# A fused attention and expert kernel: the low part of the second w1 moves to GpSimd, that of the first w2 to VectorE, and four row loads go ahead of the next weights

## The chip, the cores and the metric

The kernel runs on one core of a Trainium2 chip. The metric is device time in microseconds (us) of one execution. The kernel before took 206.73 us in the median of three executions (206.60, 206.73 and 295.39). Engines are named as the profile names them: PE is TensorE, with PEld for its weight loads; DVE is VectorE, ACT ScalarE, POOL GpSimd, SP SyncE. SP computes nothing here, it issues transfers.

## What is computed

The reference is one block on x of shape (8, 16, 16, 256): attention along the rows and the columns of each image, then a top-1 mixture of eight experts. The change touches only the second part, which in the reference, cut to its core, is

```
x = x + conv(ln(x), Wq, bq, Wk, bk, Wv, bv, Wo, bo, sigma)    # attention, per image
logits = ln(t) @ wg ; idx = argmax(softmax(logits))           # one expert per token
# each of 8 experts takes its first 256 tokens: di[e] is 256 x 256
h  = relu(einsum('ecm,emh->ech', di, w1))                     # 256 -> 1024
eo = einsum('ech,ehm->ecm', h, w2)                            # 1024 -> 256
out = t + gate * eo, back at the token's place
```

All inputs and outputs are float32. The kernel reaches the accuracy with two numbers of the fp32r type for each operand: a high part, `high = fp32r(w)`, and a low part, `low = w - high`. Each product is then three passes on PE: high by high, high by low, low by high.

## The kernel before

Two stages follow each other.

**Attention.** `sweep` runs over eight images of 256 tokens. At the end of an image POOL scatters its rows (data, gate, token number, scale) with indirect transfers into a table `slots` in device memory, ordered by expert and place (line 426). The last image is written out by hand in the VectorE block (`last_first_tile`, `last_choice`), and its two scatters are the last (`row_last`, `slot_last`).

**Experts.** For expert e the steps are:

- SP loads its 256 rows out of `slots` into `sl` (`load_slots`, line 355; 260 KB). It loads w1 of the expert (1 MB) into the one raw buffer `w1_in_sb`, and w2 (1 MB) into the one raw buffer `w2_in_sb` (lines 360, 362, then 372, 375 in the loop). A load into a raw buffer must wait until both parts of the weights that lie in it are made.
- ACT makes the high parts (`split_w1`, `split_w2`, both line 826), each in two instructions of 128x1024. They wait for the load, `w1_in` or `w2_in`.
- DVE makes the low part of w1 (line 1143) and then counts up `w1_split`; POOL makes the low part of w2 (line 456) and then counts up `w2_split`. Each is two instructions of 128x1024 too.
- DVE normalises the rows (`gathered`, line 1122, tile `xs`), PE transposes them (`gather_T`, line 690), ACT and DVE make high and low parts of the result (lines 863, 1148).
- PE multiplies by w1 (`hidden`): four groups q of two 128-wide columns of h, into four banks of PSUM. ACT makes `h_high` with the relu (line 870) and DVE `h_low` (line 1154), group by group.
- PE multiplies by w2 (`expert_out`), DVE adds the residual (line 1134) and POOL scatters the result rows into `out` (line 478).

High and low buffers are doubled (j is the parity of e); the raw buffers are single. Every engine executes its own stream in the order in which it is written, and semaphores alone tie the engines together. So an instruction that waits holds up all that stands behind it on its engine. The order on PE is: `keep_warm(36)` (line 644, products whose result nobody uses, written between the stages), `gather_T(0)`, `gather_T(1)`, `hidden(0)`, and then for each e: `hidden(e+1)`, `gather_T(e+2)`, `expert_out(e)`. ACT runs for each e the four groups of `hidden(e+1)`, with the high part of w2 of expert e+1 between the second group (q = 1) and the third, and after them the high part of the transposed rows e+2 and of w1 of expert e+2. DVE runs `gathered(e+2)`, the four groups of `hidden_low(e+1)`, `gathered_low(e+2)`, the low part of w1 of expert e+2, `output_rows(e)`.

The raw buffer of w1 is free for its third content (expert 2) when `w1_split` is 2, and that of w2 for its second content (expert 1) when `w2_split` is 1. Experts are counted from 0 in all that follows: the diff's `w2_view[1]` is expert 1.

Of the kernel before, what the change touches and what calls it, by code (L numbers as in the profile page):

```python
# [37 lines left out]
DC = D // P  # L38
NT = N // P
E, F = 8, 1024  # L40
CAP = N // E
FC = F // P
# [42 lines left out]
def wait(eng, sem, value):  # L85

    if isinstance(value, int) and value <= 0:
        return
    eng.wait_ge(sem, value)
# [18 lines left out]
def build(nc, x, Wq, bq, Wk, bk, Wv, bv, Wo, bo, sigma, wg, w1, w2, tables_in, eye, tokens, slots, out):  # L108
    f32, f32r, bf16, i32, u32 = mybir.dt.float32, mybir.dt.float32r, mybir.dt.bfloat16, mybir.dt.int32, mybir.dt.uint32
    ALU, ACT, AX = mybir.AluOpType, mybir.ActivationFunctionType, mybir.AxisListType  # L110

    ctx = ExitStack()
    with ctx:
# [6 lines left out]
        def sem(name):  # L120
            return ctx.enter_context(nc.semaphore(name))
# [12 lines left out]
        w1_in_sb, w2_in_sb = sb("w1_in_sb", [P, DC, F]), sb("w2_in_sb", [P, FC, D])  # L134
# [57 lines left out]
        w1_high, w1_low = ([sb(f"w1_{n}{j}", [P, DC, F], f32r) for j in range(2)] for n in ("high", "low"))  # L192
        w2_high, w2_low = ([sb(f"w2_{n}{j}", [P, FC, D], f32r) for j in range(2)] for n in ("high", "low"))
# [30 lines left out]
        x_in = [sem(f"x_in{j}") for j in range(len(X_GROUPS))]  # L224
        w1_in, w2_in = sem("w1_in"), sem("w2_in")
        w1_high_ready, w1_split, w2_high_ready, w2_split = (sem(n) for n in ("w1_high_ready", "w1_split", "w2_high_ready", "w2_split"))
        row_free, y_free = sem("row_free"), sem("y_free")
        slots_in = [sem(f"slots_in{j}") for j in range(2)]
        x2_stored, x2_stored_last = [sem(f"x2_stored{j}") for j in range(2)], sem("x2_stored_last")
# [45 lines left out]
        def pairs(eng, first, last, body):  # L275

            assert (last - first) % 2 == 1
            with eng.Fori(0, (last - first + 1) // 2) as turn:
                for step in range(2):
                    n = first + step  # L280
                    body(turn + n // 2, n % 2)

        def peeled(n, body, **how):
            body(n // 2, n % 2, **how)
# [20 lines left out]
        @block.sync  # L305
        def _(sp):
            def load_x(g):
                a, b = X_GROUPS[g]
                sp.dma_start(x_sb[:, a:b, :], x_view[:, a:b, :]).then_inc(x_in[g], 16)

            sp.dma_start(wk_sb, matrix(Wk)).then_inc(weights_in, 16)
            load_x(0)
            load_x(1)
            with nc.allow_non_contiguous_dma(reason="bias columns of 128"):
                sp.dma_start(bq_sb[:, :], bq.rearrange("(c p) -> p c", p=P)).then_inc(bq_in, 16)
                sp.dma_start(wg_sb[:, :, :], wg.rearrange("(c p) e -> p c e", p=P)).then_inc(wg_in, 16)
                sp.dma_start(wv_sb, matrix(Wv)).then_inc(wv_in, 16)
                for columns, b in ((bv_sb, bv), (bo_cols, bo)):
                    sp.dma_start(columns[:, :], b.rearrange("(c p) -> p c", p=P)).then_inc(small_in, 16)
            sp.dma_start(table_in[:, :], tables_in).then_inc(const_in, 16)  # L320
            load_x(2)
            sp.dma_start(w1_in_sb[:, :, :], w1_view[0]).then_inc(w1_in, 16)
            for g in range(3, len(X_GROUPS)):
                load_x(g)
            sp.dma_start(token[:, :], tokens).then_inc(token_in, 16)

            sp.sem_inc(row_free, 4)

            sp.wait_ge(xT_made, 1)
            sp.wait_ge(empty_ready, 1)  # L330
            sp.dma_start(slots_view, empty[:, None, :].to_broadcast([P, NT, RW])).then_inc(slots_empty, 16)

            sp.wait_ge(m_ready, 1)
            sp.dma_start(w2_in_sb[:, :, :], w2_view[0]).then_inc(w2_in, 16)

            def store_x2(k, j):
                sp.wait_ge(x2_ready, 2 * k + j + 1)
                sp.dma_start(out_view[:, bass.ds(4 * k + 2 * j, 2), :], row[j][:, :, 0:D]).then_inc(x2_stored[j], 16)
                sp.wait_ge(x2_stored[j], 16 * (k + 1))
                sp.sem_inc(row_free, 1)  # L340
                sp.wait_ge(row_sent[j], 32 * (k + 1))
                sp.sem_inc(row_free, 1)

            peeled(0, store_x2)

            sp.wait_ge(w1_split, 1)
            sp.dma_start(w1_in_sb[:, :, :], w1_view[1]).then_inc(w1_in, 16)
            pairs(sp, 1, B - 2, store_x2)

            sp.wait_ge(row_sent_last, 32)  # L350

            def load_slots(k, j):

                wait(sp, slots_in[j], 16 * k)
                sp.dma_start(sl[:, bass.ds(4 * k + 2 * j, 2), :], slots_view[:, bass.ds(4 * k + 2 * j, 2), :]).then_inc(slots_in[j], 16)

            peeled(0, load_slots)
            peeled(1, load_slots)
            sp.wait_ge(w1_split, 2)
            sp.dma_start(w1_in_sb[:, :, :], w1_view[2]).then_inc(w1_in, 16)  # L360
            sp.wait_ge(w2_split, 1)
            sp.dma_start(w2_in_sb[:, :, :], w2_view[1]).then_inc(w2_in, 16)
            pairs(sp, 2, E - 1, load_slots)

            sp.sem_inc(y_free, 2)

            def load_weights(k, j, w1_too=True):


                e = 2 * k + j  # L370
                sp.wait_ge(w2_split, e)
                sp.dma_start(w2_in_sb[:, :, :], w2_view[e]).then_inc(w2_in, 16)
                if w1_too:
                    sp.wait_ge(w1_split, e + 1)
                    sp.dma_start(w1_in_sb[:, :, :], w1_view[e + 1]).then_inc(w1_in, 16)
                sp.wait_ge(y_sent[j], 32 * k)
                sp.sem_inc(y_free, 1)

            pairs(sp, 2, E - 3, load_weights)
            peeled(E - 2, load_weights)  # L380
            peeled(E - 1, load_weights, w1_too=False)
            for j in range(2):
                sp.wait_ge(y_sent[j], 32 * (E // 2))
# [3 lines left out]
        def _(pool):  # L387
# [63 lines left out]
            def split_w2(n, j):  # L451

                for part in range(2):
                    pool.wait_ge(w2_high_ready, 2 * n + part + 1)
                    half = slice(part * FC // 2, (part + 1) * FC // 2)
                    step = nc.gpsimd.tensor_tensor(w2_low[j][:, half, :], w2_in_sb[:, half, :], w2_high[j][:, half, :].bitcast(f32), ALU.subtract)  # L456
                step.then_inc(w2_split, 1)
# [4 lines left out]
            peeled(B - 1, rstd2)  # L462
            peeled(B - 2, scatter_rows, tiles=[1])
            peeled(B - 1, scatter_rows)
            split_w2(0, 0)

            for j in range(2):
                pool.wait_ge(x2_stored[j], 16 * (B // 2 - j))  # L470
            pool.wait_ge(x2_stored_last, 16)
# [20 lines left out]
        def _(pe):  # L492
# [213 lines left out]
            def expert_out(k, j, last=False):  # L706

                e = 2 * k + j
                pe.wait_ge(w2_split, e + 1)
                pe.wait_ge(h_split, (FC // 2) * (e + 1))  # L710
                for t in range(2):
                    own = slice(t * P, (t + 1) * P)
                    step = three_passes(ps_y_last[t] if last else ps_y[j][:, t, :],
                                        [(h_high[j][:, f, own], h_low[j][:, f, own]) for f in range(FC)],
                                        [(w2_high[j][:, f, :], w2_low[j][:, f, :]) for f in range(FC)])
                    if last or t == 1:
                        step.then_inc(y_made, 1)
# [8 lines left out]
            peeled(0, gather_T)  # L726
            peeled(1, gather_T)
            peeled(0, hidden)
            pairs(pe, 0, E - 3, expert)
            peeled(E - 2, expert, two_on=False)  # L730
            pe.wait_ge(y_ready[1], E // 2 - 1)
            peeled(E - 1, expert_out, last=True)
# [3 lines left out]
        def _(act):  # L736
# [91 lines left out]
            def split_w1(n, j):  # L828
                split_w(w1_high, w1_in, w1_in_sb, w1_high_ready, n, j)

            def split_w2(n, j):
                split_w(w2_high, w2_in, w2_in_sb, w2_high_ready, n, j)
# [23 lines left out]
            act.wait_ge(x2_ready, B)  # L856
            act.dma_start(out_view[:, NT - 2:NT, :], row_last[:, :, 0:D]).then_inc(x2_stored_last, 16)
            peeled(B - 1, gate_exp)
            split_w2(0, 0)

            def gathered_T(k, j):
# [17 lines left out]
                    gathered_T(k + 1, j)  # L879
                    split_w1(e + 2, j)  # L880

            split_w1(1, 1)
            peeled(0, gathered_T)
            peeled(1, gathered_T)
            peeled(0, hidden)
# [5 lines left out]
        def _(dve):  # L891
# [247 lines left out]
            def split_w1(n, j):  # L1139

                for c in range(DC):
                    dve.wait_ge(w1_high_ready, DC * n + c + 1)
                    step = nc.vector.tensor_tensor(w1_low[j][:, c, :], w1_in_sb[:, c, :], w1_high[j][:, c, :].bitcast(f32), ALU.subtract)  # L1143
                step.then_inc(w1_split, 1)
# [72 lines left out]
            peeled(B - 1, place)  # L1217
            peeled(B - 1, finish_rows)

            split_w1(1, 1)  # L1220
            for n in range(2):
                peeled(n, gathered)
            for n in range(2):
                peeled(n, gathered_low)
            peeled(0, hidden_low)
            pairs(dve, 0, E - 3, expert)
            peeled(E - 2, expert, two_on=False)
            peeled(E - 1, output_rows, last=True)
# [23 lines left out]
```

## Time and profile before

| What | us |
|---|---|
| median of three executions, and the other low one | 206.73, 206.60 |
| span of the profiled execution, first to last instruction | 204.0 |
| PE busy, share of the span | 185.1 (91%) |
| VectorE busy | 146.6 (72%) |
| ScalarE busy | 105.4 (52%) |
| GpSimd busy | 102.8 (50%) |
| mean granted clock of TensorE, share of full speed | 0.961 |
| attention stage, to the last products of the last image | 0 to 89.6 |
| products of `keep_warm` between the stages | 89.6 to 100.8 |
| expert stage on PE | 102.0 to 198.6 |

The profile covers one execution. Its own device time is not listed apart from the three times; the two low ones stand 2.6 and 2.7 us over the span, and this remainder (launch and end) is taken as the same for both kernels. Of the span the profile gives the busy time of each engine, the instructions in order of time, what each idle stretch of an engine waited for, and the clock that was granted to TensorE. A row of the timeline reads: start, duration, engine, line, operation, tile written and tiles read, number of instructions merged, and in brackets the idle time ahead of it and who ended it. Two matmul instructions are issued for one float32 product, so counts of `keep_warm` are 72 for 36 products.

### The profile page before, as it was taken

Reading aid. Unit: us, or ns where it says so; the run is one execution under the profiler, and the core shown is the slowest. Engines: PE = TensorE matmul, PEld = TensorE weight load, DVE = VectorE, ACT = ScalarE, POOL = GpSimd, SP = SyncE. Lnnn points to the kernel's source line nnn. Section 1 sums busy time; section 2 is a strip of 40 time slices with the busy share of each in tenths; the row PEclk is TensorE's granted clock in tenths of the full one; section 3 lists DMA queues with packets and bytes.
Section 4 is the critical chain, followed back from the end, with each engine's and each line's share of the span. In section 5 each row is a group of like instructions: output and inputs, shape, how many; then the busy total and the mean of one; then the engine's idle time right before and its main releaser. Section 6 shows DMA issues by size and latency. Waiting matters only on the chain.

```text
span 204.0 us, 4341 instructions
## 1 busy us (share of the span) xinstructions
PE 185.1 (91%) x1404; PEld 176.7 (87%) x1404; DVE 146.6 (72%) x460; ACT 105.4 (52%) x246; POOL 102.8 (50%) x101
## 2 busy tenths in 40 slices
PE   7799399999999985959799999999999999999990
PEld 7699399998798883849789999999999999999980
DVE  0579998898999999776956584866858496465510
ACT  2368367888678644235043927538192653826000
POOL 3327574246456357558400636639183663918351
PEclk9999889999999999676999999999999999999997
DMA  5799750103712211331387639192753909271010
GB/s 186 210 394 346 223 193 0 56 0 72 292 51 83 69 60 53 105 127 51 104 310 240 178 105 345 32 367 79 235 228 113 348 16 345 96 205 42 3 55 33
DMA packets 23294, 30.86 MB, mean 151 GB/s; under 512 B 2559, under 2 KB 20113, under 8 KB 23280
## 3 DMA queue, kind: packets, MB, share of 16 engines
q1 hardware_dynamic: 20704, 25.81, 38.5%
q0 software_dynamic: 1616, 4.02, 5.5%
q10 hardware_dynamic: 960, 0.85, 1.2%
q8 instruction: 7, 0.11, 0.2%
q14 instruction: 7, 0.06, 0.1%
HBM read 22.57 MB, written 8.45 MB: 152 GB/s over the span
## 4 chain that ended last, share of the span: by engine, by line
PE 64%; DVE 22%; issue 5%; DMA 3%; ACT 2%; SPq 1%; POOLq 1%; POOL 1%; DVEq 0%; ACTq 0%
PE banks_v L506 7%; PE banks_v L513 7%; PE banks_v L507 7%; DVE w_low L1143 4%; PE bank_q L513 3%; PE bank_pT L513 3%; PE bank_pT L506 3%; PE bank_pT L507 3%; DMA wg_sb<-in_L_ffn_wg 3%; PE bank_q L506 3%; PE bank_s L513 3%; PE bank_s L506 3%; PE bank_s L507 3%; PE bank_q L507 3%; PE banks_o L580 2%
## 5 line engine op out<-in xcount | busy, mean ns | idle before, releaser
L456 POOL TENSOR_TENSOR w_low<-w_in_sb,w_high 128x1024 fp32r<-128x1024 f32 x16 | 38.4, 2421 | 17.1 <-ACT w_high L826 16.8
L478 POOL DMA_INDIRECT out<-y,goal x16 | 15.7, 979 | 35.5 <-DVE y L1134 29.1
L826 ACT ACTIVATE w_high<-w_in_sb 128x1024 fp32r<-128x1024 f32 x32 | 31.9, 1052 | 1.4 <-DMA w_in_sb<-in_L_ffn_w 1.4
L1143 DVE TENSOR_TENSOR w_low<-w_in_sb,w_high 128x1024 fp32r<-128x1024 f32 x14 | 28.1, 2044 | 4.5 <-ACT w_high L826 4.3
L426 POOL DMA_INDIRECT slots<-row,slot x14 | 14.2, 1016 | 18.1 <-DVE slot L1086 16.1
L870 ACT ACTIVATE h_high<-bank_xT 128x512 fp32r<-128x512 f32 x8 | 4.8, 597 | 28.5 <-PE bank_xT L513 28.5
L644 PE MATMUL bank_xT<-ones_wide 128*128 128x128 f32 x100 | 17.8, 360 | 1.1 <-DVE ones_wide L893 1.1
L580 PE MATMUL banks_o<-v_sb,pT 128*128 128x264 f32 x64 | 18.1, 411 | 0.6 <-DVE logit L1021 0.5
L644 PEld LDWEIGHTS bank_xT<-ones_wide 128*128 128x128 f32 x100 | 17.2, 272 | 1.1 <-DVE ones_wide L893 1.1
L506 PE MATMUL banks_v<-w_high,h_high 128*128 128x256 f32 x64 | 15.9, 287 | 0.0
L507 PE MATMUL banks_v<-w_high,h_low 128*128 128x256 f32 x64 | 15.7, 283 | 0.0
L1154 DVE SCALAR_TENSOR_TENSOR h_low<-bank_s,h_high 128x512 fp32r<-128x512 f32 x8 | 5.5, 691 | 12.6 <-ACT h_high L870 12.6
L506 PE MATMUL bank_pT<-w_high,h_high 128*128 128x256 f32 x56 | 13.9, 287 | 0.0
L507 PE MATMUL bank_pT<-w_high,h_low 128*128 128x256 f32 x56 | 13.7, 283 | 0.0
L580 PEld LDWEIGHTS banks_o<-v_sb,pT 128*128 128x128 f32 x64 | 11.5, 198 | 2.2 <-issue 0.7
L506 PE MATMUL banks_v<-m_high,xT_high 128*128 128x272 f32 x32 | 9.9, 324 | 3.4 <-DVE m_low L914 3.4
L507 PEld LDWEIGHTS banks_v<-w_high,h_low 128*128 128x128 f32 x64 | 12.3, 192 | 0.0
L506 PEld LDWEIGHTS banks_v<-w_high,h_high 128*128 128x128 f32 x64 | 12.3, 192 | 0.0
L396 POOL TENSOR_TENSOR rstd<-var_eps,minus_half 128x2 f32<-128x2 f32 (+1 forms) x6 | 4.8, 808 | 14.4 <-DVE var_eps L911 14.4
L747 ACT ACTIVATE xn<-sl,nmr,rstd 128x256 f32<-128x256 f32 (+1 forms) x16 | 8.7, 593 | 4.5 <-POOL nmr L398 4.4
L507 PEld LDWEIGHTS bank_pT<-w_high,h_low 128*128 128x128 f32 x56 | 10.7, 191 | 0.0
L506 PEld LDWEIGHTS bank_pT<-w_high,h_high 128*128 128x128 f32 x56 | 10.7, 191 | 0.0
(200 smaller groups left out, 614.5 us busy)
## 6 DMA issues: line engine op xcount, KB each, us to landing
w_in_sb<-in_L_ffn_w SPq DMA_DIRECT2D x16, 1024.0 KB
slots<-empty SPq DMA_DIRECT2D x1, 2080.0 KB, 13.7
sl<-slots SPq DMA_DIRECT2D x8, 260.0 KB, 3.2
out<-row SPq DMA_DIRECT2D x7, 256.0 KB
sl<-in_x SPq DMA_DIRECT2D x4, 256.0 KB, 6.0
sl<-in_x SPq DMA_DIRECT2D x2, 512.0 KB, 8.8
table_in<-in_tables SPq DMA_DIRECT2D x1, 292.0 KB, 6.3
w_in_sb<-in_L_conv_Wq ACTq DMA_DIRECT2D x1, 256.0 KB, 3.5
```

What stands on the lines that cost most here:

```text
L426: nc.gpsimd.indirect_dma_start(slots, bass.IndirectOffsetOnAxis(ap=slot_of(k, j)[:, t:t + 1].bitcast(u32), axis=0), row_of(k, j)[:, t, :], ...
L456: step = nc.gpsimd.tensor_tensor(w2_low[j][:, half, :], w2_in_sb[:, half, :], w2_high[j][:, half, :].bitcast(f32), ALU.subtract)
L478: nc.gpsimd.indirect_dma_start(out_rows, bass.IndirectOffsetOnAxis(ap=goal[j][:, c:c + 1].bitcast(u32), axis=0), y[j][:, c, :], None, boun ...
L506: nc.tensor.matmul(out_ap, a_h, b_h, start=c == 0, stop=False)
L507: nc.tensor.matmul(out_ap, *second, start=False, stop=False)
L513: step = nc.tensor.matmul(out_ap, *third, start=False, stop=c == n - 1)
L580: step = nc.tensor.matmul(ps_o[:, t, 0:VW], pT[:, c, t * P:(t + 1) * P], v_sb[j][:, c, :], start=c == 0, stop=c == 1)
L644: nc.tensor.matmul(ps_xT[:, 0, 0:P], ones_wide[:, :], ones_wide[:, :], start=True, stop=True)
L747: step = nc.scalar.activation(xn[:, t, :], x_sb[:, bass.ds(r, 1), :], ACT.Identity, scale=rstd[:, bass.ds(r, 1)], bias=nmr[:, bass.ds(r, 1)])
L826: nc.scalar.activation(high[j][:, half, :], raw[:, half, :], ACT.Copy).then_inc(ready, 1)
L1143: step = nc.vector.tensor_tensor(w1_low[j][:, c, :], w1_in_sb[:, c, :], w1_high[j][:, c, :].bitcast(f32), ALU.subtract)
L1154: nc.vector.scalar_tensor_tensor(h_low[j][:, 2 * q:2 * q + 2, :], ps_h[q], 0.0, h_high[j][:, 2 * q:2 * q + 2, :].bitcast(f32), ALU.max, AL ...
```

## The change

Five things change; nothing that is computed does, and no buffer is added.

1. ACT makes the high part of w1 of expert 1 ahead of the high part of w2 of expert 0 (it was the other way round).
2. POOL makes the low part of w1 of expert 1 (`second_w1_low`) in the place where it made the low part of w2 of expert 0.
3. DVE no longer makes the low part of w1 of expert 1. It makes the low part of w2 of expert 0 (`first_w2`), behind `hidden_low(0)` and ahead of its loop over the experts. A semaphore of its own, `first_w2_low`, tells of it, and `w2_split` counts from expert 1 on.
4. SP issues four loads of rows, not two, ahead of the weights of the next experts, and waits for `first_w2_low` before it loads w2 of expert 1.
5. PE has the first two turns of its expert loop written out, since expert 0 waits for another semaphore; the loop has two turns of two experts left.

```diff
-            peeled(0, load_slots)
-            peeled(1, load_slots)
+            for n in range(4):
+                peeled(n, load_slots)
             sp.wait_ge(w1_split, 2)
             sp.dma_start(w1_in_sb[:, :, :], w1_view[2]).then_inc(w1_in, 16)
-            sp.wait_ge(w2_split, 1)
+            sp.wait_ge(first_w2_low, 1)
             sp.dma_start(w2_in_sb[:, :, :], w2_view[1]).then_inc(w2_in, 16)
-            pairs(sp, 2, E - 1, load_slots)
+            pairs(sp, 4, E - 1, load_slots)
...
-                sp.wait_ge(w2_split, e)
+                sp.wait_ge(w2_split, e - 1)
...
-            split_w2(0, 0)
+            def second_w1_low():
+                for c in range(DC):
+                    pool.wait_ge(w1_high_ready, DC + c + 1)
+                    step = nc.gpsimd.tensor_tensor(w1_low[1][:, c, :], w1_in_sb[:, c, :], w1_high[1][:, c, :].bitcast(f32), ALU.subtract)
+                step.then_inc(w1_split, 1)
+            second_w1_low()
...
-                pe.wait_ge(w2_split, e + 1)
+                if isinstance(e, int) and e == 0:
+                    pe.wait_ge(first_w2_low, 1)
+                else:
+                    wait(pe, w2_split, e)
...
-            pairs(pe, 0, E - 3, expert)
+            peeled(0, expert)
+            peeled(1, expert)
+            pairs(pe, 2, E - 3, expert)
...
+            split_w1(1, 1)
             split_w2(0, 0)
...
-            split_w1(1, 1)
             peeled(0, gathered_T)
...
-            split_w1(1, 1)
+            def first_w2():
+                for part in range(2):
+                    dve.wait_ge(w2_high_ready, part + 1)
+                    half = slice(part * FC // 2, (part + 1) * FC // 2)
+                    step = nc.vector.tensor_tensor(w2_low[0][:, half, :], w2_in_sb[:, half, :], w2_high[0][:, half, :].bitcast(f32), ALU.subtract)
+                step.then_inc(first_w2_low, 1)
...
             peeled(0, hidden_low)
+            first_w2()
             pairs(dve, 0, E - 3, expert)
```

The streams at the places that matter are these. First SP, from the end of the attention stage on, before the change (`sl<-slots` are the loads of rows; of the weights 128x2x1024 is a w1 and 128x8x256 a w2):

```order
L355 DMA sl<-slots 128x2x260 [waits row_sent_last]
L355 DMA sl<-slots 128x2x260
L360 DMA w_in_sb<-in_L_ffn_w 128x2x1024 [waits w1_split]
L362 DMA w_in_sb<-in_L_ffn_w 128x8x256 [waits w2_split]
L278 UNCONDITIONAL_BRANCH
L278 ISA
L355 ISA [waits slots_in0]
L355 DMA sl<-slots 128x2x260
```

And the same place with the change:

```order
L356 DMA sl<-slots 128x2x260 [waits row_sent_last]
L356 DMA sl<-slots 128x2x260
L356 DMA sl<-slots 128x2x260 [waits slots_in0]
L356 DMA sl<-slots 128x2x260 [waits slots_in1]
L361 DMA w_in_sb<-in_L_ffn_w 128x2x1024 [waits w1_split]
L363 DMA w_in_sb<-in_L_ffn_w 128x8x256 [waits first_w2_low]
L279 UNCONDITIONAL_BRANCH
L279 ISA
L356 ISA [waits slots_in0]
L356 DMA sl<-slots 128x2x260
```

The rows of experts 2 and 3 have moved ahead of both weight loads, and the load of w2 waits for another semaphore than before.

Second DVE, behind the last slot numbers of the attention stage, before the change:

```order
L1086 SCALAR_TENSOR_TENSOR slot_last<-place_of,over 128x2 [waits place_step]
L1143 TENSOR_TENSOR w_low<-w_in_sb,w_high 128x1024 [waits w1_high_ready] x2
L1122 TENSOR_SCALAR xs<-sl 128x256 [waits slots_in0]
L1122 TENSOR_SCALAR xs<-sl 128x256
L1122 TENSOR_SCALAR xs<-sl 128x256 [waits slots_in1]
L1122 TENSOR_SCALAR xs<-sl 128x256
L1148 TENSOR_TENSOR xg_low<-banks_o,xg_high 128x512 [waits gT_ready] x2
```

With the change, the same place and on to the loop (which begins with the branch of line 279):

```order
L1096 SCALAR_TENSOR_TENSOR slot_last<-place_of,over 128x2 [waits place_step]
L1132 TENSOR_SCALAR xs<-sl 128x256 [waits slots_in0]
L1132 TENSOR_SCALAR xs<-sl 128x256
L1132 TENSOR_SCALAR xs<-sl 128x256 [waits slots_in1]
L1132 TENSOR_SCALAR xs<-sl 128x256
L1158 TENSOR_TENSOR xg_low<-banks_o,xg_high 128x512 [waits gT_ready] x2
L1164 SCALAR_TENSOR_TENSOR h_low<-bank_xT,h_high 128x512 [waits h_high_ready]
L1164 SCALAR_TENSOR_TENSOR h_low<-bank_q,h_high 128x512 [waits h_high_ready]
L1164 SCALAR_TENSOR_TENSOR h_low<-bank_s,h_high 128x512 [waits h_high_ready]
L1164 SCALAR_TENSOR_TENSOR h_low<-banks_v,h_high 128x512 [waits h_high_ready]
L1235 TENSOR_TENSOR w_low<-w_in_sb,w_high 128x1024 [waits w2_high_ready] x2
L279 UNCONDITIONAL_BRANCH
```

The pair of w_low instructions has gone from ahead of `xs`; another pair stands behind the four groups of `h_low` of expert 0.

Third ACT, in its expert loop. This place does not change, but the second row here waits for the load that SP now issues elsewhere:

```order
L881 ACTIVATE h_high<-bank_q 128x512 [waits h_made]
L832 ISA
L836 ACTIVATE w_high<-w_in_sb 128x1024 [waits w2_in]
L836 ACTIVATE w_high<-w_in_sb 128x1024
L880 REGISTER_ALU
L881 ACTIVATE h_high<-bank_s 128x512 [waits h_made]
L880 REGISTER_ALU
L881 ACTIVATE h_high<-banks_v 128x512 [waits h_made]
L873 ISA
L874 ACTIVATE xg_high<-banks_o 128x512 [waits gT_made]
L832 ISA
L836 ACTIVATE w_high<-w_in_sb 128x1024 [waits w1_in]
```

It reads: the high part of w2 of the next expert, then the third and fourth group of h, the transposed rows, and the high part of w1. The order is as before.

## Rows read from the trace of the kernel before

**Rows 1.** The chain of waits between the stages: start, duration, what.
```profile
90.87 2.85 ACT w_high L826 x3
...
93.75 7.50 DVE w_low L1143 x2
101.25 0.66 DVE xs L1122 x2
```

**Rows 2.** Timeline of PE from `keep_warm` to `hidden` of expert 2.
```profile
89.62 11.21 PE L644 MATMUL bank_xT<-ones_wide 128*128 128x128 f32 x72
101.95 1.30 PE L690 MATMUL banks_o<-ident,xs 128*128 128x128 f32 x8 [1.12 <-DVE xs L1122]
...
109.39 0.28 PE L506 MATMUL bank_xT<-xg_high,w_high 128*128 128x256 f32 x1
...
115.50 0.36 PE L506 MATMUL banks_v<-w_high,h_high 128*128 128x256 f32 x1
...
121.34 0.30 PE L506 MATMUL bank_xT<-xg_high,w_high 128*128 128x256 f32 x1
```

**Rows 3.** The tile w_low, 88 to 150 us: duration in ns, min/median/max.
```profile
L456 POOL TENSOR_TENSOR w_low<-w_in_sb,w_high x9: 2384/2421/2435, 94.3 to 150.0; 128x1024 fp32r<-128x1024 f32 x9
L1143 DVE TENSOR_TENSOR w_low<-w_in_sb,w_high x8: 1210/1524/6367, 93.7 to 143.8; 128x1024 fp32r<-128x1024 f32 x8
```

**Rows 4.** Timeline of POOL: low parts of w2, experts 0 and 1.
```profile
94.28 4.75 POOL L456 TENSOR_TENSOR w_low<-w_in_sb,w_high 128x1024 fp32r<-128x1024 f32 x2
114.09 4.81 POOL L456 TENSOR_TENSOR w_low<-w_in_sb,w_high 128x1024 fp32r<-128x1024 f32 x2 [15.06 <-ACT w_high L826]
```

**Rows 5.** Timeline of SP, the issues; then from issue to landing of the row loads.
```profile
96.17 0.91 SPq L355 DMA_DIRECT2D sl<-slots  x2
...
101.69 0.47 SPq L362 DMA_DIRECT2D w_in_sb<-in_L_ffn_w  x1
...
119.08 0.38 SPq L372 DMA_DIRECT2D w_in_sb<-in_L_ffn_w  x1
121.29 0.38 SPq L375 DMA_DIRECT2D w_in_sb<-in_L_ffn_w  x1
...
178.68 0.37 SPq L372 DMA_DIRECT2D w_in_sb<-in_L_ffn_w  x1
...
DMA to landing us min/median/max: 2.7/3.2/7.6
```

**Rows 6.** Timeline of DVE: last h_low of expert 0, then low part of w1, expert 2.
```profile
110.22 0.69 DVE L1154 SCALAR_TENSOR_TENSOR h_low<-banks_v,h_high 128x512 fp32r<-128x512 f32 x1 [0.75 <-ACT h_high L870]
...
117.41 3.71 DVE L1143 TENSOR_TENSOR w_low<-w_in_sb,w_high 128x1024 fp32r<-128x1024 f32 x2
```

**Rows 7.** Timeline of ACT: w2 of expert 1, then w2 and w1, one expert later.
```profile
112.96 2.00 ACT L826 ACTIVATE w_high<-w_in_sb 128x1024 fp32r<-128x1024 f32 x2
...
124.92 2.00 ACT L826 ACTIVATE w_high<-w_in_sb 128x1024 fp32r<-128x1024 f32 x2
...
129.00 2.01 ACT L826 ACTIVATE w_high<-w_in_sb 128x1024 fp32r<-128x1024 f32 x2 [0.61 <-DMA w_in_sb<-in_L_ffn_w]
```

**Rows 8.** Busy time by stretch, the last w2 load: stretch, engines, PEclk, DMA share, GB/s.
```profile
179.50:181.00 1.50, 1.50 (x15) 1.50 (x14) 1.45 (x3) 0.00 (x0) 0.00 (x0) 1.00 0.85 136
181.00:182.50 1.50, 1.50 (x15) 1.50 (x14) 0.88 (x2) 0.00 (x0) 0.00 (x0) 1.00 1.01 354
...
183.00:183.50 0.50, 0.50 (x7) 0.50 (x6) 0.14 (x1) 0.33 (x1) 0.31 (x1) 1.00 0.74 240
```

**Rows 9.** The same view around two idle stretches of PE (first engine column).
```profile
20.40:23.86 3.46, 0.03 (x2) 0.00 (x1) 3.46 (x3) 1.88 (x6) 2.75 (x1) 1.00 0.99 300
23.86:27.50 3.64, 3.64 (x17) 3.64 (x18) 3.54 (x17) 0.68 (x3) 1.41 (x3) 0.53 0.64 202
...
86.90:89.40 2.50, 0.07 (x1) 0.00 (x0) 2.40 (x16) 0.23 (x2) 1.07 (x2) 0.91 0.32 111
...
89.40:95.70 6.30, 6.24 (x33) 6.25 (x34) 2.94 (x10) 4.46 (x8) 5.10 (x5) 0.50 0.29 100
```

More of the change, by code:

```diff
@@ L226, in build @@
         w1_high_ready, w1_split, w2_high_ready, w2_split = (sem(n) for n in ("w1_high_ready", "w1_split", "w2_high_ready", "w2_split"))
+        first_w2_low = sem("first_w2_low")
         row_free, y_free = sem("row_free"), sem("y_free")
```

## The prediction, as written before the result

> **What bounds the kernel now.** I read the chain of waits first. Through the experts it is PE, one matmul behind the other. Between the stages it leaves PE: four small ACT instructions, ACT's high parts of both weights, 7.50 us of DVE on two low parts, then `xs`, then the transposes [rows 1]. So the change works on a stretch of the chain. The timeline of PE tells how much lies there: the products of `keep_warm` run from 89.62 to 100.83, and only the 1.12 us behind them are idle [rows 2]. The reader should see that the chain names DVE for 7.50 us, while PE has other work in its stream for all but 1.12 of them.
>
> Why DVE takes 7.50 us is in the tile's view: one of its low parts takes 1.21 us at best and 6.37 at most [rows 3]. The long one began at 93.75 and POOL's two instructions ran from 94.28 to 99.03 [rows 4]: DVE got on only when POOL was through. Later it is alike: the pair that began at 117.41 ended at 121.12, 2.22 us after POOL's pair ended at 118.90 [rows 6, 4]. I reckon 2.4 us for a pair of DVE that is alone, and 2.2 us past the end of POOL's pair for one that meets it.
>
> **The head of the expert stage.** Without the pair on DVE, `xs` waits only for the rows. Their loads are issued at 96.17 and land 2.7 to 3.2 us later at the usual, so at 98.9 to 99.4 [rows 5]. Two `xs` take 0.66 us on the chain, so they are ready by 100.1. PE is free at 100.83 and no sooner, since `keep_warm` stays. Gain: 101.95 - 100.83 = **1.1 us**. It would be 0 if the rows landed at 101.2 or later (the longest landing shown, 7.6 us, is of a load that ran beside two weight loads), and it can't exceed 1.12.
>
> POOL's pair costs as much on w1 as on w2, the same shape, 4.75 us: `w1_split` is 2 at 99.0, not 101.25, and PE needs it for `hidden(1)`, which began at 109.39 [rows 2] and would now at 108.3. Free. The swap of ACT's high parts costs nothing: three of the four are done by 93.72 [rows 1], the fourth about 1 us later, and nothing but POOL's pair waits there. The row loads of experts 2 and 3 ahead of w1 of expert 2 put that load at about 100; before, it went out just ahead of the w2 at 101.69 [rows 5], so it is not late. PE's two written-out turns add rows to its stream and no matmul; no row prices them, and I take 0, since the loop's turns already join without a gap in the same timeline.
>
> **The load of w2 of expert 1: the term that decides.** Before, it was issued at 101.69 [rows 5] and ACT read it at 112.96 [rows 7], 11.3 us later. Now the raw buffer is free only when `first_w2` is done, and that stands behind `hidden_low(0)`. Its last group ran from 110.22 to 110.9 [rows 6]; with the 1.1 us of the head, to 109.8. Add a DVE pair alone, 2.4 us: SP issues the load at **112.2**. ACT comes to its wait after q = 1, at 112.96 - 1.1 = 111.9. The load cannot be there: it isn't even issued.
>
> How long does 1 MB take from issue to landing? Below: the last w2 was issued at 178.68 [rows 5], and its data flow until close to 183.5, first at 136 GB/s, then at 354, and still at 240 in the half microsecond from 183.0 [rows 8]; so not under 4.7 us. Above: w1 of expert 3, issued at 121.29 behind a w2, ended ACT's wait at 129.00 [rows 5, 7], 7.7 us. Between: w2 of expert 2, issued at 119.08, was there when ACT read it at 124.92 without a wait, so in 5.84 us at most. I take 5.8, since that is the same kind of load, and now 0.5 MB of rows for experts 4 and 5 are issued right behind. Landing at **118.0**.
>
> The Trainium skill (DMA: Bandwidth & Descriptors, Anatomy of one DMA) gives about 2.0 us fixed and the bytes by 436 GB/s; for 1 MB that makes 4.4 us as an estimate, and the result would be 1.4 us lower than mine. Rows 8 speak against it, with data still moving 4.3 to 4.8 us after the issue, and the measurement decides.
>
> **What is queued behind the wait.** On ACT, behind the high part of w2, stand the third and fourth group of `h_high`, the transposed rows, and the high part of w1 of expert 2. DVE's low part of that w1 needs it, and `hidden(2)` on PE needs that. POOL's low part of w2 of expert 1 starts as soon as ACT has its first half, so it collides with DVE's pair, as before. All this is one pattern, and its length is in the trace: ACT began w2 at 112.96 and DVE ended the low part of w1 at 121.12 [rows 7, 6], 8.2 us. PE started `hidden(2)` at 121.34, at once behind `expert_out(0)` [rows 2], so 0.2 us was all the slack there was. Now: 118.0 + 8.2 = **126.2**. PE has `hidden(1)`, `gather_T(2)` and `expert_out(0)` until 121.34 - 1.1 = 120.2 (`expert_out(0)` began at 115.50 [rows 2], now at 114.4, and `first_w2` is done at 112.2: free). PE then stands idle for **6.0 us**. Net against before: 126.2 - 121.34 = **+4.9 us**. With the load's bounds, +3.8 to +6.8.
>
> Behind that the old rhythm returns, late by this sum: the w2 load of expert 2 is issued when POOL is done, 2.3 us before `hidden(2)` starts, as before, and DVE's `y_free` has been given by then.
>
> **The clock.** After PE idled for 3.4 us (20.4 to 23.86) the next 3.6 us ran at a mean of 0.53, after 2.5 us (86.9 to 89.4) the next 6.3 us at 0.50 [rows 9]: the lower of its two levels, 1.2 GHz instead of 2.4. So I expect the same behind 6.0 us of idle. What it costs is half of the slow stretch: 3.4/2 = 1.7 us or 6.3/2 = 3.15 us. Neither row is nearer, I take the middle, **2.4 us**. PE is the bound there, so nothing hides it.
>
> **Sum.** The profiled execution has 204.0 us of span; 204.0 + 4.9 + 2.4 = 211.3, and with the 2.7 us around the span **214.0 us**, 3.5% slower. 204.0 + 2.7 is 206.7, the median of the three runs, so one sum serves for both. The bounds of the two unknown costs together give 206.7 + 3.8 + 1.7 = 212.2 to 206.7 + 6.8 + 3.15 = 216.7.
>
> **Rivals.**
> - *The wait comes, the clock stays.* PE loses only the 6.0 us of idle: 211.6 us, at the load's bounds 210.5 to 213.5. For it: nothing in the rows; against it: both idle stretches ahead of slow ones, and shorter ones at that [rows 9]. 0.07.
> - *Not slower: the load is hidden.* The head's 1.1 us is all that is left, 205.6 us. The place is ACT's wait at q = 1. With the price of the clock at 1.7 us, the kernel would be within 2% (4.1 us) of before only if the load landed within 3.4 us of its issue, and it would gain only if ACT's wait were over by 113.0, 0.8 us after the issue. Against it stand the 4.7 us of rows 8, and DVE's order, which puts `first_w2` behind h_low. 0.05.
> - *The transfers pile up.* The row loads of experts 4 and 5 run beside w2 of expert 1, and the later weight loads, issued in the same spacing, lose their small slack (ACT waited 0.61 us for one already [rows 7]). Then the landing takes 7.7 us or more and a wait or two of 0.5 to 1 us follow: 216 to 218 us. 0.12. The Trainium skill (DMA: Bandwidth & Descriptors, Queues, rings and completion order) says that each DMA engine consumes the descriptors of a ring in order, so rows issued behind w2 should not delay it; by that this rival would not come, and no row here shows a load that was issued alone ahead of rows.
> - *The change does not do what it says at the head.* The rows land late or `xs` meets POOL's pair, and PE starts no sooner: 214.0 + 1.1 = 215.1 us. POOL's pair ends at 99.0, before the rows are there, which speaks against it. 0.08.
>
> My forecast has 0.68. The range should leave out 2 in 10: it runs from the lower case with the clock up, 210.6, to the piled-up transfers, 216.9. A measurement of this kernel can tell about 2% from no change, that is 202.6 and 210.9. Slower than that: the forecast, the head and the pile-up in full, and most of the case with the clock up: 0.92. Within 2%: the hidden load and the rest, 0.07. Faster by over 2% would need 4.1 us, and only 1.1 us of idle is there to remove: 0.01.
>
> **What would show it.** (1) PE's transposes of expert 0 start at about 100.8, directly behind `keep_warm`. (2) DVE's pair of w_low between 109.8 and 112.2, with 1.2 us for each. (3) SP issues w2 of expert 1 at about 112.2; ACT has a wait of about 6 us for it between the second and third group of expert 1, ended by the transfer. (4) PE is idle for about 6 us before `hidden(2)`, ended by DVE's w_low, and the granted clock is 0.5 for 3 to 6 us behind it. (5) From there on every expert takes the 11.96 us of before (112.96 to 124.92 on ACT [rows 7]). The forecast falls if the load lands in under 4 us, or if POOL's pair and DVE's don't meet (then `hidden(2)` comes up to 1.5 us sooner).

## The result

The changed kernel is slower: 213.18 us in the median (212.91 to 215.20), the kernel before 206.71 on the same chip, a ratio of 1.0295 with an interval of 1.0224 to 1.0366. I had forecast 214.0 us and a ratio of 1.035. Each ratio in this document is estimated from those executions of both kernels that lie near their fastest, so it need not be the quotient of the medians. Executions of one kernel spread by 1 to 2%: the changed kernel from 212.91 to 215.20, the kernel before, on another chip, from 205.78 to 210.13. In the one kernel that was profiled twice, most of the difference lies in the attention stage, where TensorE's granted clock was low for longer in one of the two (see the first experiment). So the argument below goes by stretches of one profiled execution, and the times are given beside them.

Three numbers of each profile carry it. The first product of `keep_warm` between the stages marks the end of attention on PE. From there to the first transpose of the expert stage is the *head*. From that transpose to the end of the span is the *expert stretch*.

| Kernel | keep_warm starts | head | expert stretch | span |
|---|---|---|---|---|
| before | 89.62 | 12.33 | 102.05 | 204.0 |
| changed | 90.54 | 9.99 | 110.47 | 211.0 |
| difference | +0.92 | -2.34 | +8.42 | +7.0 |

The expert stretch lost 8.4 us and the head gave 2.3 back. The 0.9 us ahead of both is attention, where nothing was changed. The spans differ by 7.0 us and the medians by 6.5, most likely because the span of 204.0 does not belong to an execution of 206.7 us: in all 33 executions of the kernel before for which the record has both numbers, on other chips, the time is 1.74 to 1.88 us over the span, not 2.7.

**PE.** This is the timeline of PE in the changed kernel; the lines of the second stage are shifted, line 690 of before is 695. It answers to [rows 2].

```profile
90.54 9.90 PE L649 MATMUL bank_xT<-ones_wide 128*128 128x128 f32 x72
100.53 1.42 PE L695 MATMUL banks_o<-ident,xs 128*128 128x128 f32 x8
...
118.97 1.12 PE L518 MATMUL banks_v<-w_low,h_high 128*128 128x256 f32 x8
125.69 0.58 PE L511 MATMUL bank_xT<-xg_high,w_high 128*128 128x256 f32 x1 [5.60 <-DVE w_low L1153]
```

The transposes now stand right behind `keep_warm`, 0.09 us later. Between `expert_out` of expert 0 and `hidden` of expert 2, where 121.34 had followed without a gap, PE is idle for 5.60 us and DVE's w_low ends it.

**The chain.** The chain of waits (start, duration, what) says what DVE waited for in its turn. It answers to [rows 1].

```profile
96.96 2.75 DMA sl<-slots
99.73 0.73 DVE xs L1132 x2
...
110.55 1.23 DVE w_low L1235
111.80 5.71 DMA w_in_sb<-in_L_ffn_w
...
118.50 1.04 ACT w_high L836
...
124.42 1.22 DVE w_low L1153
125.69 0.58 PE bank_xT L511
```

Read it from the bottom: PE waits for DVE's low part of w1, that for ACT, ACT for the transfer, the transfer for VectorE's `first_w2` (line 1235). In the kernel before no transfer stood in this part. ACT's and POOL's timelines show the same wait from their side:

```profile
111.06 0.60 ACT L881 ACTIVATE h_high<-bank_q 128x512 fp32r<-128x512 f32 x1 [0.84 <-PE bank_q L518]
117.53 2.01 ACT L836 ACTIVATE w_high<-w_in_sb 128x1024 fp32r<-128x1024 f32 x2 [5.88 <-DMA w_in_sb<-in_L_ffn_w]
...
120.88 2.01 ACT L836 ACTIVATE w_high<-w_in_sb 128x1024 fp32r<-128x1024 f32 x2
```

```profile
95.21 4.74 POOL L470 TENSOR_TENSOR w_low<-w_in_sb,w_high 128x1024 fp32r<-128x1024 f32 x2
118.67 4.75 POOL L457 TENSOR_TENSOR w_low<-w_in_sb,w_high 128x1024 fp32r<-128x1024 f32 x2 [18.72 <-ACT w_high L836]
```

Compare the pair of ACT at 117.53 with [rows 7]: w2 of expert 1 began at 112.96 without a wait on a transfer, now at 117.53 after 5.88 us. The rest of the pattern is a copy: POOL's pair starts 1.14 us behind it, as it did before, 114.09 against 112.96 [rows 4, 7].

**The clock.** Busy time by stretch: the columns are those of [rows 8], the first number behind the stretch's length is PE.

```profile
120.10:125.70 5.60, 0.01 (x1) 0.01 (x1) 5.57 (x7) 2.79 (x4) 3.32 (x2) 0.91 0.35 105
125.70:131.30 5.60, 5.60 (x26) 5.60 (x27) 2.13 (x6) 0.68 (x2) 1.97 (x2) 0.50 1.03 356
131.30:132.30 1.00, 1.00 (x10) 1.00 (x10) 0.45 (x1) 1.00 (x2) 0.00 (x0) 0.91 0.33 132
```

After 5.6 us of idle PE works for 5.6 us at 0.50, the level of 1.2 GHz: 26 matmuls in 5.6 us, where the next microsecond alone has 10. That costs 5.6/2 = 2.8 us. With the idle time it is 8.4 us, which is all that the expert stretch lost.

### The profile page after: what moved, and what is told of

It is laid out like the page before. It is cut to its first block, busy times and chain, and to the rows that moved or that the text cites. A ratio compares the mean times of both kernels' runs of the same rounds, so it can differ in the third digit from the quotient of the medians.

```text
span 211.0 us, 4318 instructions
## 1 busy us (share of the span) xinstructions
PE 186.5 (88%) x1404; PEld 177.1 (84%) x1404; DVE 139.9 (66%) x460; ACT 106.5 (50%) x246; POOL 102.8 (49%) x101
## 4 chain that ended last, share of the span: by engine, by line
PE 52%; DVE 22%; DMA 9%; issue 8%; POOL 3%; ACT 3%; DVEq 1%; SPq 1%; POOLq 1%; ACTq 0%
PE banks_v L518 5%; PE banks_v L511 5%; PE banks_v L512 5%; DVE prob L1012 4%; DMA wg_sb<-in_L_ffn_wg 3%; PE bank_pT L518 3%; PE bank_pT L511 3%; PE bank_pT L512 3%; PE bank_q L511 3%; DMA w_in_sb<-in_L_ffn_w 3%; PE bank_q L518 3%; PE bank_q L512 3%; PE bank_s L511 2%; PE bank_s L512 2%; PE bank_xT L511 2%
## 5 line engine op out<-in xcount | busy, mean ns | idle before, releaser
L457 POOL TENSOR_TENSOR w_low<-w_in_sb,w_high 128x1024 fp32r<-128x1024 f32 x14 | 33.6, 2420 | 23.6 <-ACT w_high L836 23.6
L1153 DVE TENSOR_TENSOR w_low<-w_in_sb,w_high 128x1024 fp32r<-128x1024 f32 x12 | 19.5, 1659 | 2.9 <-ACT w_high L836 2.7
L585 PE MATMUL banks_o<-v_sb,pT 128*128 128x264 f32 x64 | 17.5, 399 | 0.6 <-DVE logit L1031 0.5
L649 PE MATMUL bank_xT<-ones_wide 128*128 128x128 f32 x100 | 15.4, 327 | 1.1 <-DVE ones_wide L903 1.1
L649 PEld LDWEIGHTS bank_xT<-ones_wide 128*128 128x128 f32 x100 | 15.0, 242 | 1.1 <-DVE ones_wide L903 1.1
L511 PE MATMUL bank_xT<-xg_high,w_high 128*128 128x256 f32 x32 | 9.2, 308 | 5.6 <-DVE w_low L1153 5.6
L585 PEld LDWEIGHTS banks_o<-v_sb,pT 128*128 128x128 f32 x64 | 11.0, 189 | 2.2 <-issue 0.7
L512 PEld LDWEIGHTS banks_v<-w_high,h_low 128*128 128x128 f32 x64 | 12.3, 192 | 0.0
L511 PEld LDWEIGHTS banks_v<-w_high,h_high 128*128 128x128 f32 x64 | 12.3, 192 | 0.0
L511 PEld LDWEIGHTS bank_xT<-xg_high,w_high 128*128 128x128 f32 x32 | 6.6, 206 | 6.0 <-DVE w_low L1153 5.8
L1132 DVE TENSOR_SCALAR xs<-sl 128x256 f32 (+1 forms) x16 | 5.9, 408 | 7.8 <-DMA sl<-slots 7.7
```

The lines of the kernel that those rows point to most:

```text
L511: nc.tensor.matmul(out_ap, a_h, b_h, start=c == 0, stop=False)
L512: nc.tensor.matmul(out_ap, *second, start=False, stop=False)
L585: step = nc.tensor.matmul(ps_o[:, t, 0:VW], pT[:, c, t * P:(t + 1) * P], v_sb[j][:, c, :], start=c == 0, stop=c == 1)
L649: nc.tensor.matmul(ps_xT[:, 0, 0:P], ones_wide[:, :], ones_wide[:, :], start=True, stop=True)
```

## The experiments

All start from the changed kernel. "Before" is always the kernel before on the same chip, 207.7 to 208.1 us in the median. The changed kernel itself was not run on those chips, so the experiments are compared with it by the ratio and by the expert stretch.

### The first w2's low part earlier

```diff
-            peeled(0, hidden_low)
             first_w2()
+            peeled(0, hidden_low)
```

> The changed kernel, with one move: VectorE makes the first w2's low part ahead of the four groups of h_low of expert 0, not behind them. My theory (the loss is ScalarE's wait for the load of w2 of expert 1, plus the slow clock behind TensorE's idle time): the pair now ends near 105.6, the load is issued there, lands 5.7 us later at 111.3, ScalarE asks at 111.6, so nobody waits and TensorE never idles; the time is 205.6 to 206.5 us, at or just under the kernel before. Rival A (the loss is VectorE's extra pair as such, or TensorE's two written-out turns): both are still there, so most of the 6.5 us stays, 211 to 213 us.

It took 206.91 us in the median, before 207.96. One execution took 203.38 us and three 206.62 to 207.35, too few to tell more, so I repeated it.

> The run with the first w2's low part ahead of h_low, repeated, since it had but one undisturbed time (203.38 us). My theory: the whole loss is the late issue, so this is 205 to 206.5 us, 0.5 to 2.5 us under the kernel before on the same chip. Rival A (VectorE's extra pair or TensorE's written-out turns cost by themselves): 208 us or more.

Measured: 203.54 us (202.95 to 207.37), before 207.74, ratio 0.9804 with an interval of 0.9745 to 0.9863. The ten executions of this kernel fall into two groups, five from 202.95 to 203.80 us and five from 206.62 to 207.37, and the ratio speaks of the lower group. The first profile is of the upper group (207.35 us) and the second of the lower (203.15). Their spans differ by 4.3 us, and 3.5 of them are attention, which ends at 92.70 and at 89.18: in the first the granted clock was 0.51 from 11 to 21 us, in the second 1.00. Where it matters the two agree: the expert stretch is 102.13 and 102.03 us, that of before is 102.05. This is the timeline of SP and then of ACT in the second one:

```profile
104.12 0.38 SPq L363 DMA_DIRECT2D w_in_sb<-in_L_ffn_w  x1
```

```profile
110.18 2.00 ACT L836 ACTIVATE w_high<-w_in_sb 128x1024 fp32r<-128x1024 f32 x2
```

The load has 6.06 us and ACT does not wait. All 8.4 us are gone while VectorE's extra pair and TensorE's two written-out turns are still there: neither costs anything here, and rival A falls. From the start of `keep_warm` to the end this version takes 112.0 and 112.8 us in its two profiles, the kernel before 114.4 and the changed kernel 120.5. So it is about 8 us shorter there than the changed kernel and 1.6 to 2.4 us shorter than the kernel before, all of that in the head. I can't trace the rest of the ratio of 0.98 to the change: it lies ahead of `keep_warm`, or in executions that have no profile.

### Half way

```diff
-            peeled(0, hidden_low)
+            peeled(0, hidden_low, groups=(0, 1))
             first_w2()
+            peeled(0, hidden_low, groups=(2, 3))
```

> The changed kernel, with VectorE's pair between the second and the third group of h_low of expert 0. My theory: the load is issued at 109.0, lands at 114.7, hidden of expert 2 starts 8.2 us after that, 122.9, with 2.9 us of idle TensorE before it; 208.0 to 208.5 us if the clock stays up, up to 211 if it falls. The loss follows the time of the issue. Rival A (the extra pair as such): 213 us, as it is the same work in another place. Rival B (a fixed penalty once any wait occurs): 213 us too.

209.22 us (208.20 to 212.06), ratio 1.0068 (0.9978 to 1.0158). Its expert stretch is 107.36 us, 5.3 over before. Two lines of its timelines, SP and ACT, and one of PE:

```profile
107.62 0.37 SPq L363 DMA_DIRECT2D w_in_sb<-in_L_ffn_w  x1
```

```profile
114.28 2.01 ACT L836 ACTIVATE w_high<-w_in_sb 128x1024 fp32r<-128x1024 f32 x2 [3.92 <-DMA w_in_sb<-in_L_ffn_w]
```

Here the load took 6.66 us, not 5.7, so that PE was idle for 3.7 us and not the 2.9 I had worked out, and the granted clock was 0.50 for about 3.3 us behind it. Why this load took longer stays open. The loss follows the time at which the load is issued and lands; a fixed penalty is excluded by 107.36 against 110.47.

### TensorE kept busy while it waits

```diff
             peeled(0, expert)
+            pe.wait_ge(h_split, FC // 2 + 1)
+            keep_warm(30)
             peeled(1, expert)
```

> The changed kernel, with 30 products of keep_warm on TensorE between expert_out of expert 0 and hidden of expert 2, where it idles. They take 5.0 us at full clock and end before VectorE's low part is there, so the 5.6 us are lost as before, but not idle. My theory: only the cost of the clock goes, 2.8 us by the trace of the changed kernel (5.6 us at half), so 210.2 to 210.8 us. Rival (the slow clock is paid by slack elsewhere, or the products themselves delay hidden): 213 us or more.

210.72 us (209.87 to 211.66), ratio 1.0158 (1.008 to 1.0236). The time is in my range, but the products took 6.86 us and not 5.0:

```profile
120.13 6.86 PE L649 MATMUL bank_xT<-ones_wide 128*128 128x128 f32 x60
126.74 0.37 PE L511 MATMUL bank_xT<-xg_high,w_high 128*128 128x256 f32 x1
```

DVE's low part was ready at 125.8, so they held PE up for 0.9 us. The expert stretch is 108.86 us, above the 107.7 of the theory, so the time fell into my range partly by luck. With 22 products:

> The changed kernel with 22 products of keep_warm in TensorE's idle time, not 30: 30 took 6.9 us and ended 0.9 us after VectorE's low part. 22 take 5.0 us and end before it. My theory: the clock stays up and only the 5.6 us of waiting are lost, so from the transposes of expert 0 to the end it takes 107.7 us (before 102.05, changed kernel 110.5), and the time is 210 us. Rival (the clock is no part of the loss): 110 us or more for that stretch.

210.67 us (209.65 to 210.92), ratio 1.0147 (1.0084 to 1.021), and an expert stretch of 108.05 us against 110.47. The clock over the same stretch as above:

```profile
120.10:125.70 5.60, 5.11 (x46) 4.92 (x44) 5.32 (x5) 3.07 (x5) 3.63 (x2) 1.00 0.35 109
125.70:131.30 5.60, 5.30 (x44) 5.30 (x45) 3.13 (x8) 2.72 (x4) 2.46 (x3) 1.00 1.01 347
```

It stays at 1.00, and 2.4 us of the 2.8 come back, although the wait is as long as ever. So the clock is a term of its own, about a third of the loss.

### Both low parts on GpSimd

```diff
             second_w1_low()
+            for part in range(2):
+                pool.wait_ge(w2_high_ready, part + 1)
+                half = slice(part * FC // 2, (part + 1) * FC // 2)
+                step = nc.gpsimd.tensor_tensor(w2_low[0][:, half, :], w2_in_sb[:, half, :], w2_high[0][:, half, :].bitcast(f32), ALU.subtract)
+            step.then_inc(first_w2_low, 1)
...
-            first_w2()
```

> The changed kernel, but GpSimd makes both low parts, w1 of expert 1 and then w2 of expert 0; VectorE makes neither. The load of w2 of expert 1 is issued near 104.8 and lands before ScalarE asks, so its wait is gone in every theory. What this run tells is whether VectorE's xs (one input, SBUF to SBUF) is held up by GpSimd as its two-input subtraction was: if so, xs starts only at 104.7, TensorE idles 4 us behind keep_warm, and the time is 209.5 to 212 us. If xs is not held up: 205.6 to 206.5 us.

209.90 us (209.50 to 213.80), ratio 1.0111 (1.0031 to 1.0191): `xs` is held up. The tile's view of xs in this kernel (ns, min/median/max), and POOL's pair of w2:

```profile
L1137 DVE TENSOR_SCALAR xs<-sl x4: 399/400/4412, 99.3 to 104.3; 128x256 f32<-128x256 f32 x4
```

```profile
98.94 4.66 POOL L477 TENSOR_TENSOR w_low<-w_in_sb,w_high 128x1024 fp32r<-128x1024 f32 x2
```

The first xs began at 99.34 and was done when POOL was, at 103.6. It has one tensor input only, so not just the subtraction of two tensors suffers, as [rows 3] could have been read. The head grew to 14.59 us, and the expert stretch by 1.4 us over before, because the clock fell behind 3.41 us of idle PE (0.50 from 106 to 109). No load was waited for.

### Both low parts on VectorE

```diff
-            second_w1_low()
...
+            split_w1(1, 1)
+            first_w2()
             for n in range(2):
                 peeled(n, gathered)
...
-            first_w2()
```

> The changed kernel, but VectorE makes both low parts (w1 of expert 1, then w2 of expert 0) ahead of xs, and GpSimd makes none. VectorE was idle for 7 to 8 us there, waiting for the rows. If its subtractions take 1.2 us each when GpSimd computes nothing, all four are done before the rows land, the weight loads go out early, nobody waits for w2 of expert 1, and only the wait between the stages is gone: 204.5 to 206 us, 1 to 2 us under the kernel before on the same chip. Rival: VectorE's pairs hold up GpSimd's last scatters (or are held up by them), so that the rows land late: 207 us or more.

206.80 us (205.42 to 209.60), ratio 0.9972 (0.9935 to 1.001): no difference, between what I and the rival had said. All four of DVE's instructions took 1.2 us, but the rival's mechanism was at work. The timelines of POOL and DVE in this kernel:

```profile
94.69 1.91 POOL L427 DMA_INDIRECT slots<-row_last,slot_last  x1 [0.69 <-issue]
96.90 1.97 POOL L427 DMA_INDIRECT slots<-row_last,slot_last  x1 [0.30 <-issue]
```

```profile
94.53 2.36 DVE L1152 TENSOR_TENSOR w_low<-w_in_sb,w_high 128x1024 fp32r<-128x1024 f32 x2 [0.72 <-ACT w_high L835]
96.81 2.35 DVE L1234 TENSOR_TENSOR w_low<-w_in_sb,w_high 128x1024 fp32r<-128x1024 f32 x2
```

The last two scatters take 1.91 and 1.97 us beside VectorE; in the changed kernel they take 0.97 and 0.98. VectorE's pairs began first here, at 94.53 and 96.81. In the kernel before, the second scatter began at 93.29, ahead of VectorE's subtraction (93.75), and took 0.97. The row loads go out 7.94 us after the start of `keep_warm`, against 6.42 in the changed kernel and 6.02 in the second profile of the first experiment, and the head is 11.72 us.

That is still 0.6 us shorter than before, but the expert stretch is 103.5 us, 1.4 over before, and it took the gain away: the granted clock fell behind the 1.84 us that PE idled for the rows and was 0.50 from 106 to 109, 2 us after PE had started again. The idle time alone doesn't say when this happens: in the first experiment it was 1.71 us, and the clock stayed at 1.00. (This profile is of the longest of the twelve executions, 209.60 us.)

> As the run in which VectorE makes both low parts, and keep_warm between the stages has 31 products, not 36. If the end of keep_warm is what now holds TensorE back between the stages, this gains up to 1.1 us more, where the clock came up late; if the rows (landing, then xs) are what holds it back, it gains nothing: the same as that run. Rival: with fewer products the clock falls or comes up later, and it is slower by 1 to 3 us.

208.10 us (205.67 to 209.77), ratio 1.0002 (0.9958 to 1.0047), head 11.62 us, 0.1 us less. `keep_warm` was not what PE waited for there, the rows were. The granted clock was 0.50 here too behind 1.52 us of idle PE, and the expert stretch 104.1 us. The interval of the ratio overlaps with that of the run with 36, so whether fewer products also cost something stays open.

### The row loads

```diff
-            for n in range(4):
+            for n in range(2):
                 peeled(n, load_slots)
...
-            pairs(sp, 4, E - 1, load_slots)
+            pairs(sp, 2, E - 1, load_slots)
```

> The changed kernel with the fourth part undone: two row loads ahead of the weights, as before the change, the others behind the load of w2 of expert 1. The rows of expert 2 then go out only at 112.6, behind 1 MB, and VectorE's xs for them, ahead of h_low of expert 1 in its stream, waits until about 118. My theory: TensorE now idles before the transposes of expert 2 and expert_out of expert 0, 5 us, and hidden of expert 2 still starts near 125.7 to 126.5, because ScalarE's wait for w2 ends at the same time: 213 to 214 us, the wait has another place and the same size. Rival (the waits add up): 218 us or more.

215.38 us in two runs, ratio 1.0365 (1.0215 to 1.0516), above my 213 to 214. The wait did change its place, but it also grew, to 9.65 us of idle PE:

```profile
122.34 1.11 PE L695 MATMUL banks_o<-ident,xs 128*128 128x128 f32 x4 [9.65 <-DVE xs L1132]
```

```profile
117.34 4.94 DVE L1132 TENSOR_SCALAR xs<-sl 128x256 f32 x2 [6.78 <-DMA sl<-slots]
```

```profile
117.43 4.70 POOL L457 TENSOR_TENSOR w_low<-w_in_sb,w_high 128x1024 fp32r<-128x1024 f32 x2 [18.64 <-ACT w_high L836]
```

The late rows let xs meet POOL's pair, which holds it up by 4 us: what the both-on-GpSimd run showed, and what I left out of the expectation. (The load of w2 itself took 5.71 us here, as in the changed kernel.) So the fourth part of the change is worth 3.1 us of the expert stretch (113.58 against 110.47) while the load of w2 is as late as this.

```diff
-            for n in range(4):
+            for n in range(E):
                 peeled(n, load_slots)
...
-            pairs(sp, 4, E - 1, load_slots)
```

> The changed kernel with all eight row loads ahead of the weights, so that w2 of expert 1 moves alone. In the changed kernel it took 5.7 us from issue to the end of ScalarE's wait, with two row loads issued right behind it. If rows behind a load delay it, it now takes 4.8 to 5.2 us and the loss shrinks by 0.5 to 0.9 us; if not, it takes 5.6 to 5.9 us and the time is that of the changed kernel, 212.5 to 213.5 us. I expect the second, because the rows of the kernel before show a load with nothing behind it whose data flow for 4.3 to 4.8 us after the issue, before any completion.

213.42 us in two runs, ratio 1.0271 (1.0144 to 1.0399), expert stretch 110.17 us. The load, issued at 112.60, ended ACT's wait at 118.75: 6.15 us with no rows behind it, longer than I had said and not shorter. So nothing speaks for a delay by the rows. But this is one load, five others with rows behind them took 5.69 to 6.66 us, and the load of w1 had gone out only 4.8 us ahead of it here (10.9 us in the changed kernel) and still moved data when it was issued. So an effect of half a microsecond is not excluded.

## Why the prediction was right

**The late load: right, and nearly its size.** Forecast: issue at 112.2, landing at 118.0 after 5.8 us, 8.2 us more to `hidden` of expert 2, 6.0 us of idle PE. Measured: 111.80, 117.53 (5.7 us), 8.16 us more, 5.60 us. Over the five other runs in which somebody waited for this load it took 5.69 to 6.66 us. Moving the issue earlier removed all of it; half way removed part. The pile-up of transfers did not come: with row loads behind it 5.7 us, alone 6.15, and no other wait of PE in the expert stretch. The 4.4 us that the prediction set beside it from the Trainium skill (DMA: Bandwidth & Descriptors, Anatomy of one DMA — SWDGE (gpsimd) path) come from a fit for transfers that GpSimd issues, and SyncE issues this one. None of the six took less than 5.69 us, and the measurement decides.

**The clock: right in kind.** I took 2.4 us, the middle of 1.7 and 3.15; it was 2.8 in the profiled execution, and 2.4 came back when TensorE was kept busy. The rival "the clock stays" fell.

**The head: mis-sized.** "PE is free at 100.83 and no sooner, since `keep_warm` stays. Gain: 1.1 us" gave the right start for the wrong reason. The transposes did start at 100.53, right behind `keep_warm`, but that had started 0.92 us later and took 9.90 us, not 11.21. Its length is no constant: the same 72 matmuls took 11.21 us with 6 us of them at the half clock (before), 9.90 with 3.4 us (changed), and 8.28 in the second profile of the first experiment, at the full clock throughout. So the head gave 2.3 us and not 1.1. Where `keep_warm` took 8.28 us, in four profiles, PE waited 1.6 to 1.7 us more for the rows, and the head was 9.9 to 10.0 us: that is what the scatters, the row loads and xs need, and the real bound (it was 10.7 in the first profile of that kernel, whose row loads went out 1.0 us later). The term "it can't exceed 1.12" was wrong. Worked out from these profiles, the gain is 12.3 us less the longer of `keep_warm` and 10.0, 1.1 to 2.3 us, by how long the clock is low in `keep_warm`, which the change doesn't touch.

**The span: right in part by luck.** I had forecast 211.3 us and it was 211.0, but the terms were further off than their sum. Against before, the idle time of PE came to 5.6 us and not 6.0, the clock to 2.8 and not 2.4, the head to -2.3 and not -1.1, and attention, for which I had nothing, to +0.9. Each pair nearly cancels.

**What lies around the span** was 1.9 us in the changed kernel (212.91 with a span of 211.0), and I had taken 2.7, out of a span and times that most likely don't belong together. So for this execution the forecast was 1.1 us too high: 0.3 in the span and 0.8 here.

**The parts at no cost** were at no cost, taken together: with the load early, the expert stretch is within 0.1 us of before, with TensorE's written-out turns, the swapped order on ACT and VectorE's extra pair in it.

## What to carry to other kernels

Before a step is moved to where its engine is idle, ask which buffer it frees and which transfer waits for that; here a pair of 2.35 us in a gap of VectorE cost 8.4 us of the expert stretch, because 1 MB that had been issued 11 us ahead of its use now was issued when ScalarE already asked for it, and moving the same pair to a place 6.3 us earlier won everything back. Count with an idle stretch of TensorE the half clock behind it: 5.60 us idle were followed by 5.6 us at 0.50, which cost 2.8 more, and 3.68 us idle by about 3.3 at 0.50. Behind short ones, 1.5 to 1.9 us, the clock fell in some runs and stayed up in others. And an idle engine is no free engine where it shares a path: VectorE and GpSimd held each other up in both directions.

## What was not expected of the hardware

- VectorE's `xs`, a one-input instruction of 400 ns from SBUF to SBUF, took 4.4 us beside GpSimd's subtractions. It began at 99.34, during the first of GpSimd's pair, and was done only at the end of the second, 103.6: VectorE did not get in between the two. It can, though: in the run with two row loads ahead, the first of two xs began at 117.34, took 2.60 us and ended just after the second of GpSimd's instructions had begun; the other xs then took 2.42. The Trainium skill (Trainium Architecture — The Big Picture, What this means for kernel authors) calls the port pair that these two engines share an exclusive lock and not a split of bandwidth. The traces agree: 4412 against 400 ns, and in [rows 3] 6367 against 1210.
- It works the other way as well: GpSimd's indirect scatters took 1.91 and 1.97 us beside VectorE's two-input subtractions that had begun ahead of them, 0.97 without.
- VectorE's `h_low`, which reads one operand from PSUM, took 0.69 us with and without GpSimd beside it (120.06, with POOL's pair from 118.67 on, against 0.69 at 108.81).
